# One block for two layers, early loads, and a last image that stays on chip

## The reference

```python
# layer 0: in 8 groups of 8 channels, all products of two and of three channels of the group
p2 = x[:, :, _I2] * x[:, :, _J2]
y2 = einsum('bgihw,goi->bgohw', p2, W2) + b2
p3 = x[:, :, _I3] * x[:, :, _J3] * x[:, :, _K3]
y3 = einsum('bgihw,goi->bgohw', p3, W3) + b3
l = x + y2 * beta2 + y3 * beta3 * 0.1
# layer 1, n images, 3136 pixels each
g = clip(bn(conv1x1(l, w_inside), gamma1, beta1, mean1, var1), 0, 6)
theta = l[:, :32]
f = einsum('niab,nicd->nabcd', theta, theta)        # 3136 x 3136 scores an image
f = softmax(f.reshape(n, 3136, 56, 56), axis=1)     # first over one pixel index,
f = softmax(f.reshape(n, 3136, 3136), axis=2)       # then over the other
out = einsum('nabcd,nicd->niab', f, g) / 56 * 56
out = bn(depthwise_conv3x3(out, w_dw), gamma2, beta2, mean2, var2) + l
```

## Time and profile before

| | us |
|---|---|
| median of 3 runs | 5472.18 (5471.32 to 5474.18) |
| profiled execution | 5471.45 |
| its span, first to last instruction | 5469.6 |
| PE busy | 5270.9 (96%) |
| ACT busy | 5136.6 (94%) |
| DVE busy | 4458.1 (82%) |
| POOL busy | 4448.5 (81%) |

### The profile page before, as it was taken

One profiled execution on the slowest core, in us unless ns is written; L12 is line 12 of the kernel. 1 busy time (PEld: TensorE's weight loads), 2 busy tenths in 40 slices (PEclk: granted clock), 3 DMA queues, 4 the chain that ended last, 5 costly groups with the idle time before them and its releaser, 6 DMA issues.

```text
span 5469.6 us, 91044 instructions
## 1 busy us (share of the span) xinstructions
PE 5270.9 (96%) x33410; PEld 2671.4 (49%) x33410; DVE 4458.1 (82%) x8965; ACT 5136.6 (94%) x3029; POOL 4448.5 (81%) x1849
## 2 busy tenths in 40 slices
PE   8999969999999999999999999999999999999995
PEld 3444435555555555454555454555555455545442
DVE  7888867888888888888888888888888888888885
ACT  7888859999999999999999999999999999999995
POOL 5666635888888898989888888888888888898886
PEclk9999979999999999999999999999999999999998
DMA  7777751222222222222222222222222222222211
GB/s 148 162 165 161 161 109 27 55 56 51 57 60 61 60 60 60 61 61 59 54 61 53 59 48 55 57 58 58 57 52 55 61 61 60 61 61 60 60 37 37
DMA packets 231224, 382.53 MB, mean 70 GB/s; under 512 B 161981, under 2 KB 179582, under 8 KB 220542
## 3 DMA queue, kind: packets, MB, share of 16 engines
q1 hardware_dynamic: 230782, 376.70, 33.1%
HBM read 260.16 MB, written 103.56 MB: 66 GB/s over the span
## 4 chain that ended last, share of the span: by engine, by line
PE 77%; issue 4%; DVE 3%; ACT 1%; DMA 0%; SPq 0%; POOL 0%; DVEq 0%; POOLq 0%
PE at_AV L963 41%; PE at_S L932 23%; PE at_AV L969 11%; DVE at_ring L836 2%; PE at_AV L959 2%; DVE at_ZACC L900 0%; ACT at_ring L781 0%; DVE at_OUTB L867 0%; ACT at_ring L787 0%; DMA at_YT<-yd 0%; DMA rzd<-at_ZC 0%; DMA at_ZB<-rzd 0%; DVE at_RZ L853 0%; DMA out<-at_OUTB 0%; SPq L673 0%
## 5 line engine op out<-in xcount | busy, mean ns | idle before, releaser
L836 DVE TENSOR_SCALAR_CACHE_REDUCE at_ring<-at_S 128x1176 f32<-128x1176 f32 (+1 forms) x2352 | 2889.7, 1242 | 436.9 <-PE at_S L932 409.1
L745 POOL TENSOR_TENSOR at_ZP<-at_ZP,at_ring 128x1568 f32<-128x1568 f32 x640 | 2282.8, 3608 | 292.5 <-ACT at_ring L787 277.7
L781 ACT ACTIVATE at_ring<-at_ring,at_NM 128x3136 f32<-128x3136 f32 x784 | 2279.3, 2907 | 127.5 <-DVE at_NM L845 117.4
L963 PE MATMUL at_AV<-at_ring,at_GT 128*64 128x392 f32 x12800 | 2323.9, 504 | 37.5 <-issue 34.3
L787 ACT ACTIVATE at_ring<-at_ring,at_RZ 128x3136 f32<-128x3136 f32 x784 | 2273.5, 2900 | 0.0
L932 PE MATMUL at_S<-at_THM,at_THS 128*128 128x392 f32 x6144 | 1464.0, 366 | 85.9 <-DVE at_ring L836 42.7
L963 PEld LDWEIGHTS at_AV<-at_ring,at_GT 128*64 128x64 f32 x12800 | 862.1, 137 | 1149.0 <-issue 1085.6
L932 PEld LDWEIGHTS at_S<-at_THM,at_THS 128*128 128x128 f32 x6144 | 1031.8, 190 | 757.3 <-DVE at_ring L836 493.6
L758 POOL TENSOR_TENSOR at_OUTB<-at_OUTB,at_ZB 128x1568 f32<-128x1568 f32 x248 | 885.2, 3569 | 16.9
L969 PE MATMUL at_AV<-at_ring,at_ones 128*32 128x392 f32 x7168 | 663.7, 498 | 0.0
L458 DVE TENSOR_TENSOR l_U<-l_TY,l_XB 128x448 f32<-128x448 f32 x896 | 497.1, 618 | 99.4 <-PE l_TY L498 99.4
(11 more groups left out here) (70 smaller groups left out, 2466.8 us busy)
## 6 DMA issues: line engine op xcount, KB each, us to landing
l_X<-in_x SPq DMA_DIRECT2D x128, 392.0 KB, 7.4
at_THM<-hld SPq DMA_DIRECT2D x128, 392.0 KB, 6.4
at_THS<-hld SPq DMA_DIRECT2D x256, 192.0 KB, 4.0
at_CIN<-att SPq DMA_DIRECT2D x64, 406.0 KB, 7.0
at_ZB<-rzd SPq DMA_DIRECT2D x64, 406.0 KB, 5.1
yd<-l_YO SPq DMA_DIRECT2D x128, 196.0 KB, 5.5
att<-at_ACC SPq DMA_DIRECT2D x256, 98.0 KB
at_OUTB<-yd SPq DMA_DIRECT2D x64, 392.0 KB, 8.0
```

The source lines that it names most:

```text
L745: e.tensor_tensor(z, z, v, ALU.add).then_inc(g_add, 1)
L781: e.activation(v, v, ACT.Exp, bias=NM[:, i:i + 1], accum_out=ZS[:, i:i + 1]).then_inc(a_p1, 1)
L836: e.tensor_scalar(ring[:, s % RING, QC * a_:QC * b].rearrange("p (b w) -> p b w", w=QC), PS[:, k % 2, 0:b - a_, 0:QC], 1.0, None, ALU.mult ...
L963: ins = e.matmul(dst[64 * j:64 * j + 64, 0:QC], GT[fl.n % 2][:, keys_of(fl.n, t), :], ring[:, slot, q:q + QC], start=(t == GROUPS[fl.i][0] ...
```

## The change

- **One block.** `layer0` returns its parts for each engine, and `attention` calls them inside its own block. Attention's constants and small buffers (THM, THS, THL, YT, GT and so on) get room beside layer 0's; ring, ACC, ZACC, OUTB, CIN, ZB and ZP take layer 0's room when it is done. In place of the meeting of all engines stand waits: `read` (TensorE, for the last VectorE and ScalarE steps of layer 0), `stored` (POOL before it clears CIN and ZB, VectorE before the first copy to ACC or ZACC, for the last stores).
- **Order of the start.** SP issues image 0 first, then six constants of layer 0, then images 1 to 3; ScalarE's queue issues attention's four and layer 0's other six constants. VectorE's memsets and constants for attention, with the square roots on ScalarE, run ahead of layer 0.
- **Early loads.** In layer 0's SP order, after image 8 (`EARLY`), stand the first loads of attention: THM, THS of image 0, THL of images 0 and 1, all four YT of image 0. Two of the YT batches lie in THM[1] for that; THM of image 1 waits until they are used.
- **Fills of image 0.** Its "g" batches may start after the first tile's scores (`b // 2`), not ahead of them.
- **The last image.** Its last group is split (tiles 22, 23, then 24 alone, with z ahead of o). VectorE takes the reciprocal of ZACC itself; eight matmuls with a 0/1 matrix (`spread`) broadcast it over the partitions into PSUM; VectorE multiplies ACC with it, straight into CINL. For that an o fill now takes the slices j and j + 4 (rows of the upper and the lower half of the image) instead of 2j and 2j + 1, in all images. Two copies inside SBUF bring the halo rows. VectorE convolves 21 of 28 rows of each half (`SHARE`), POOL seven; each part is stored by itself.

The core of the diff:

```diff
+LAST_GROUPS = GROUPS[:-1] + [range(22, 24), range(24, 25)]
...
-            pre.append(Fill("g", n, b, 0, f if n else -1, f + 3 if n else -1))
+            pre.append(Fill("g", n, b, 0, f if n else b // 2, f + 3 if n else b // 2 + 1, n_img))
...
+    def stored(e):
+        for n in range(max(0, n_img - 2), n_img):
+            e.wait_ge(s_st[n % 2], 64 * (n // 2 + 1))
+            e.wait_ge(s_hl[n % 2], 128 * (n // 2 + 1))
+
+    def read(e):
+        e.wait_ge(a_s, 3 * NU)
+        e.wait_ge(v_t, y_use(NU - 1) + 1)
...
+            if n == min(EARLY, n_img - 1):
+                for i in range(min(2, n_img - 1)):
+                    e.wait_ge(s_st[i], 64)
+                    e.wait_ge(s_hl[i], 128)
+                early()
...
+            def last_out():
+                e.wait_ge(v_bd, 3)
+                e.wait_ge(v_sc, 2)
+                e.dma_start(CINL[64:128, 0, 1:57], CINL[0:64, 28, 1:57]).then_inc(s_halo, 16)
+                e.dma_start(CINL[0:64, 29, 1:57], CINL[64:128, 1, 1:57]).then_inc(s_halo, 16)
+                for done, r0, r1 in ((v_fin, 0, SHARE), (g_fin, SHARE, 28)):
+                    e.wait_ge(done, 1)
+                    for h in range(2):
+                        e.dma_start(out[last, :, HW // 2 * h + W * r0:HW // 2 * h + W * r1],
+                                    OUTL[64 * h:64 * h + 64, W * r0:W * r1]).then_inc(s_out, 16)
...
+            def early():
+                e.wait_ge(g_ms, 7)
+                thm(0)
+                for h in range(2):
+                    ths(0, h)
+                for n in range(min(2, n_img)):
+                    thl(n)
+                e.wait_ge(v_ms, 3)
+                for b in range(4):
+                    yt(0, b)
+
+            l0_sync(e, early)
...
+            def last_rows():
+                O3 = OUTL.rearrange("p (r w) -> p r w", w=W)[:, SHARE:28, :]
...
+                for k_, v in enumerate(CENTRE_FIRST):
+                    i, j = divmod(v, 3)
+                    if k_ == 3:
+                        e.wait_ge(s_halo, 32)
+                    link(e.tensor_scalar(T3, CINL[:, SHARE + i:28 + i, j:j + 56], w9[:, v:v + 1], 0.0, ALU.mult, ALU.add))
+                    ins = e.tensor_tensor(O3, O3, T3, ALU.add)
...
+            def last_recip(i):
+                e.wait_ge(v_ev, index["z", last, len(groups(last, n_img)) - 1, i] + 1)
+                e.reciprocal(ZACC[:, i, :], ZACC[:, i, :]).then_inc(v_rl, 1)
+
+            def last_rows():
...
+                for k_ in (0, 3, 1, 2):
+                    e.wait_ge(pe_b, k_ + 1)
+                    if k_ == 0:
+                        e.wait_ge(v_ev, len(fills))
+                    e.tensor_tensor(CINL[:, 1 + 7 * k_:8 + 7 * k_, 1:57], ACC[:, k_, :].rearrange("p (r w) -> p r w", w=W),
+                                    PS[:, k_ // 3, k_ % 3, 0:QC].rearrange("p (r w) -> p r w", w=W), ALU.mult)\
+                     .then_inc(v_sc, 1)
...
-                        q = QC * (2 * fl.j + j)
+                        q = QC * (4 * j + fl.j)
...
-            e.wait_ge(g_ms, 9)
-            e.wait_ge(v_ms, 2)
+            l0_tensor(e)
+            l0_read(e)
+            e.wait_ge(g_ms, 7)
+            e.wait_ge(v_ms, 3)
...
+            e.wait_ge(v_rl, 2)
+            for k in range(4):
+                for h in range(2):
+                    ins = e.matmul(PS[64 * h:64 * h + 64, k // 3, k % 3, 0:QC], spread[:, k, :], ZACC[:, h, :],
+                                   start=True, stop=True)
+                ins.then_inc(pe_b, 1)
```

More of the change, by code:

```diff
@@ L22 @@
 CH = HW // NCH
+EARLY = 8
 NT = 25
@@ L38 @@
 LAT = 60
+SHARE = 21
+CENTRE_FIRST = (3, 4, 5, 0, 1, 2, 6, 7, 8)
 SUM = -1
@@ L55, in tiles_of, with groups, group_of, __init__ @@
     return ([(2 * p, r)] if r < NT else []) + ([(2 * p + 1, r - NT + 1)] if r >= NT - 1 else [])
[L58 to L63, removed]
+def groups(n, n_img):
+    return LAST_GROUPS if n == n_img - 1 else GROUPS
+def group_of(n, t, n_img):
+    return next(g for g, r in enumerate(groups(n, n_img)) if t in r)
 class Fill:
-    def __init__(self, kind, n, i, j, first, last):
+    def __init__(self, kind, n, i, j, first, last, n_img):
         self.kind, self.n, self.i, self.j, self.first, self.last = kind, n, i, j, first, last
-        tiles = BATCHES[i] if kind == "g" else GROUPS[i]
+        tiles = BATCHES[i] if kind == "g" else groups(n, n_img)[i]
         width = {"g": 1, "o": 2, "z": 4}[kind]
@@ L530, in attention @@
-def attention(nc, a, yd, hld, out, n_img):
     pe_order, dve_order, pool_order, fills, ended, _ = plan(n_img)
@@ L565, in attention @@
         w9 = sb("w9", [128, 9])
+        memory = ExitStack()
+        with memory:
+            l0_sync, l0_gpsimd, l0_scalar, l0_vector, l0_tensor, l0_stored, l0_read = layer0(
+                nc, ctx, memory, a, x, yd, hld, n_img)
+        ring = sb("ring", [128, RING, HW])
+        ACC = sb("ACC", [128, 4, QC])
+        ZACC = sb("ZACC", [128, 2, QC])
+        OUTB = sb("OUTB", [128, HW // 2])
+        CIN = sb("CIN", [128, 30, 58])
+        ZB = sb("ZB", [128, 30, 56])
+        ZP = sb("ZP", [128, HW])
+        last = n_img - 1
+        OUTL = GT[1 - last % 2][:, :, :].rearrange("p t c -> p (t c)")[:, 0:HW // 2]
+        CINL = ZP[:, 0:30 * 58].rearrange("p (r w) -> p r w", w=58)
+        spread = THL[:, :, :].bitcast(F32).rearrange("p i (k c) -> p (i k) c", c=64)
         PS = ctx.enter_context(nc.psum_tensor("at_S", [128, 2, 3, 512], F32))
@@ L738, in add @@
                 e.wait_ge(a_p2, s + 1)
+                if n == last and t == POOLED[0] and h == 0:
+                    if n:
+                        e.wait_ge(pe_s, NP * (base(n - 1) + NT))
+                    e.memset(spread[:, :, :], 0.0).then_inc(g_cl, 1)
+                    e.wait_ge(g_cl, 1)
+                    for j in range(4):
+                        e.memset(spread[32 * j:32 * j + 1, j, :], 1.0).then_inc(g_cl, 1)
+                        e.wait_ge(g_cl, 2 + j)
                 if t == POOLED[0]:
```

629 lines of the change are left out of this document (337 added, 292 removed).

## The result

Median of 4 runs: 5434.98 us (5430.27 to 5443.06), against 5471.75 us of the kernel before, measured beside it (5465.56 to 5474.18). The ratio is 0.9936, 95% interval [0.9919, 0.9953]. It is faster by 36.8 us, where 60 were forecast; 5434.98 lies above the range of 5393 to 5427. The profiled execution took 5436.95 us, its span 5435.1.

The account below looks back on a forecast made before the run. Attention is bound by TensorE and ScalarE, layer 0 by TensorE, so gains come only where both stand still. Terms -52 + 0 + 13 - 21 = -60 on 5471.45 give 5411, with the median's 0.7 5412 us; range 5393 to 5427.

Parts of the forecast that it names:

- The start: Up to the first selection matmul: all twelve constants there near 15 us, selection at 19.8 as now; 0 us.
- The bound of +2: Upper bound of the term for the kernel's start, which was 0 us; the lower was -2.6.
- The tail: After the last exponentials: split last group, reciprocals and spreads on chip, shared convolution end the span earlier; -21 us.
- the price of a tap: Last image's convolution: VectorE 1.47 us a tap, POOL 1.02 and 0.59 plus 0.17 between; nine taps 13.3 and 16.0 us.
- POOL 20% slower: End of the kernel: with half clock throughout, the case behind the bound of -17 us on a gain of -21.
- The stall: Layer 0, image 9: early loads delay the TH copies on SP's in-order queue, so TensorE rests once; +13 us.
- rival 1: Layer 0: the early loads cost nothing, TH not held up or slack found; 5399 us, chance 0.20.
- if only issue time counted: Layer 0: bound on the early loads' cost from SP's 24 issues of some 0.5 us alone; 8 us.
- Between the layers: Layer 0's last sum to attention's continuous work: block boundary gone, first loads on chip, exponentials and output work earlier; -52 us.
- Rival 3: Between the layers: something else of the first tile is late, half of the 52 us remains; 5438 us, chance 0.04.
- Rival 2: Layer 0 or first tiles: longer issues, image 10 or 11 also hit, or lasting half clock; about 5428 us, chance 0.15.
- Rival 4: Attention: o matmuls slower from ring columns farther apart, 11 ns on 6400 eating 73 us; slower than before, chance 0.03.

Follow-up runs that it names:

- start_wait: Changed kernel, but SP holds images 1 to 3 back until the twelve constants have landed; 5433.01 us in one run.
- start_sp: Changed kernel, but SP issues all twelve constants of layer 0 ahead of image 0; 5425.61 us, ratio 0.9914.
- tail_psum: Changed kernel, but VectorE keeps its running sum of the last image's taps in PSUM, with rows and taps as they were; 5428.94 us, ratio 0.9927.
- issue_only: Changed kernel, but 24 tiny loads replace the early loads, and the real ones come after layer 0; 5473.96 us in one run.
- gt_late: Changed kernel, but the four GT batches of image 0 may start two tiles later; 5443.93 us in one run.
- best_gt: Changed kernel plus constants first on SP, early loads spread over images 8 to 21, VectorE's sum in PSUM with 24 rows, image 0's GT batches two tiles later; 5396.92 us.

## Why the prediction was wrong, and where it was right

The direction of the total and the mechanism of the gap and of the stall held; the start's step and the price of the tail's taps failed, and all four terms were off to the same side. By the cut the span lacks 25.5 us of the forecast: 11.5 at the start, 8.9 in the tail, 3.5 in the stall, 2.2 between the layers, less 0.5 in the steps of attention.

**The start (0, measured +11.5) is the step that failed.** It added up bytes, 2.6 MB at 200 GB/s, and concluded that all twelve constants are there near 15. That treats two queues as one pipe that is served in the order of issue. But ScalarE's last constants, issued from 5.75 on, compete with twelve image DMAs issued on SP from 6.33 on, and land at 22.8. With those twelve held back (`start_wait`) they are there at 14.84, so the bytes themselves were added up rightly. The Trainium skill ("DMA: Bandwidth & Descriptors", Queues, rings and completion order) says that each DMA engine alternates between the queues at the grain of packets. By it a queue of many small packets beside one of large ones gets few bytes; the traffic of the first 30 us agrees in the main (DMA queues: packets, MB, share of 16 engines; q1 is SP's, q10 ScalarE's):

```profile
q1 hardware_dynamic: 1341, 5.84, 89.1%
q10 hardware_dynamic: 1182, 0.37, 7.7%
```

From 6 to 22.8 us each queue moved 1070 packets, SP's 3.45 MB in them and ScalarE's 0.30. Equal turns don't tell all of it: from 15 us on it was 203 packets against 64, and why ScalarE's last ones came so seldom isn't shown. The bound of +2 had no row behind it at all. The chain, priced at its old 3.54 us, was also moved beside POOL's first splits and took 7.1. From the 15 of the forecast to 22.8 and from 3.54 to 7.1, that is the 11.5. `start_sp` removes both parts; `start_wait` removes the wait and keeps the slow chain. Attention's own constants were also later than forecast, done at 15.75 and not by 10; the wait for `be` hid that here, and in `start_wait` it cost 2.6 us.

**The tail (-21, measured -12.1).** Its path was right almost everywhere. From the last exponential to the four products 23.3 us were forecast, 1 for the half clock among them, and 22.9 measured, with 1.4 for it. The reciprocals took 2.60 us where I had 2.7. (The estimate from the Trainium skill, "VectorE: DVE Perf Modes", First, the fixed hardware budget, was 3.3: the measurement decides.) What failed is the price of a tap. POOL's 1.02 and 0.59 came from rows of layer 0 and were right for POOL alone; VectorE's 1.47 likewise (1.45 in `tail_psum`). Side by side, with two SBUF inputs on VectorE, they are 2.01, 1.60 and 1.85. The bound of "POOL 20% slower" was a guess. The rows of layer 0 couldn't tell of exclusion, since VectorE's products beside them take one of their inputs from PSUM (l_TY, which TensorE writes). With the exclusion gone the tail is 42.09 us, at full clock; the forecast's was 42.3 with 1 us for the half clock. (Its sum has a slip of 0.2: 5444.4, two issues of 0.55 and 2.1 make 5447.6.)

**The stall (+13, measured +16.5).** Place, cause and single occurrence were right, and rival 1 is out. Its price by bytes nearly held: from the first early load's issue to TH it had 24.4 us (248.11 to 272.5), and the trace has 25.9 (260.16 to 286.02). Of the 3 us by which the rest was longer than 12.3, 1.5 are this. Another 1.3 come from SP, which got to the early loads that much later after image 8's TH copies than before (19.35 instead of 18.09 us), and 0.5 from slack that wasn't there. The half clock cost 1.1 where I took 1. The term lay within its own bounds of 0 and 20, and the bound "if only issue time counted", 8, is what `issue_only` measured: a rest of 8.2.

**Between the layers (-52, measured -49.8).** The first exponential came 4.7 us after the last sum, as worked out. The step that put the GT batches "into time in which TensorE waits for VectorE" forgot that VectorE evacuates them; `gt_late` shows that 1.9 of the 2.2 us went there. That the gap came out so near is in part luck: it was 10.3 us in most traces, 13.7 and 14.2 in the two in which the clock fell early. Output work started 39 us after the last sum where I had 32. ScalarE ran on without a break until some 60 us after it, and the steps as a whole took no longer than before.

**The rivals.** Rival 3 (half of the gap stays) would give 5438, near the measured time, and is false: the gap closed. Rival 2 (5428) had longer trouble in layer 0, but no second image was hit, and the clock was back at 1.00 within 5 us of the end of the rest. Rival 4 (whose 11 ns on 6400 matmuls would be 70 us, not 73) is out by the line of the page, with 504 ns as before the change:

```profile
L963 PE MATMUL at_AV<-at_ring,at_GT 128*64 128x392 f32 x12800 | 2323.9, 504 | 37.5 <-issue 34.3
```

```profile
L1096 PE MATMUL at_AV<-at_ring,at_GT 128*64 128x392 f32 x12800 | 2325.2, 504 | 39.3 <-issue 33.3
```

The range failed because it was built from the cases of one term: it let the stall vary and left the start and the tail at their middle values, though the tail's own bounds reached 4 us up.

**Open.** The clock falls 4 to 5 us after the last sum in `start_wait`, `tail_psum` and `gt_late`, some 13 after it in the changed kernel and some 20 in `best_gt`. Why it does so I did not settle. In the first two the code between the layers is the changed kernel's, so no edit explains it. The early fall costs some 4 us in the first tiles.

## What to carry to other kernels

Price a moved transfer by its queue and what stands on the other queues at that moment, not by total bytes: small constants go ahead of bulk loads, and early loads are dealt out behind the copies that someone waits for. When work is split between VectorE and GpSimd, first ask where each reads: durations from rows with another neighbour didn't hold here, and one operand in PSUM made both run at full speed. A DMA put into an in-order queue costs its issue time, and on top of it what is left of its transfer when the issues are done.

## What the runs showed of the hardware that was not expected

- Two loads of 64 KB on ScalarE's queue took 8.6 and 16.5 us to land beside image loads of 392 KB each on SP's, and 2.6 to 3.8 us on SP's ahead of them.
- VectorE's two-input taps and POOL's SBUF operations slow each other: POOL 0.59 to 1.60 and 1.01 to 2.01 us, VectorE 1.45 to a mean of 1.85. The pair together was slower than VectorE alone with all rows (25.2 us against 16.95).
- A tiny load costs SP as much as a large one: 24 of them took 12.3 us of the queue's time (262.22 to 274.56), the 24 real ones 12.6 (260.16 to 272.79).
- The granted clock fell to 0.50 some 4 to 20 us after the last sum of layer 0. Among traces with the same code between the layers it fell early in two, and there the second exponential came 3.4 to 3.9 us later.
- The reciprocal of 392 float32 elements a partition took 2.60 us, 6.6 ns an element.
